# Token stage of a graph and expert network on one core: other softmax batches, VectorE copies, and every third group's down product moved into the first pass

## The reference

```python
logits = x @ gate_w                       # 16 experts
probs = softmax(logits, axis=-1)
scores, tok = top_k(probs.T, 625)         # per expert, over all 10000 tokens
y = (gelu(x[tok] @ w1 + b1) @ w2 + b2) * scores
routed = zeros_like(x).at[tok].add(y)
shared = gelu(x @ sw1 + sb1) @ sw2 + sb2  # hidden size 64
out = routed + shared
```

## Time and profile before

| what | value |
|---|---|
| median of 3 runs | 4557.2 us (4544.28 to 4563.69) |
| profiled execution, its own time | 4542.55 us |
| its span, first to last instruction | 4540.8 us |
| mean granted TensorE clock | 0.912 |
| busy share: TensorE, VectorE, ScalarE, GpSimd | 90%, 62%, 46%, 33% |
| token stage, first pass | 1308.7 to 1470 us |
| token stage, search and second pass | 1475.7 to 1583 us |
| clock granted in the steps / in the search | 0.99 / 0.50 |
| table loads of ScalarE in the stage | 16, of 1283 ns |
| copies of Q by ScalarE | 40, median 357 ns |

### The profile page before, as it was taken

One profiled execution on the slowest core, in us unless ns is written; L12 is line 12 of the kernel. 1 busy time (PEld: TensorE's weight loads), 2 busy tenths in 40 slices (PEclk: granted clock), 3 DMA queues, 4 the chain that ended last, 5 costly groups with the idle time before them and its releaser, 6 DMA issues. The chain is left out here.

```text
span 4540.8 us, 65002 instructions
## 1 busy us (share of the span) xinstructions
PE 4084.8 (90%) x22630; PEld 3319.3 (73%) x22630; DVE 2802.7 (62%) x5418; ACT 2085.5 (46%) x3584; POOL 1497.0 (33%) x1431
## 2 busy tenths in 40 slices
PE   7888999889977968789999999998899998999967
PEld 3447788777766656549988589886699874998844
DVE  5665666569965677568844445443555435557888
ACT  1222233333357334265567533575434764335566
POOL 1442266228820758654400333102332004330010
PEclk9998999999988578799999999998999998999965
DMA  8985488449964879765423655225653237545677
GB/s 308 402 330 178 159 293 267 174 142 376 390 229 146 316 151 178 158 220 158 155 74 116 219 167 158 93 104 164 206 158 113 94 123 238 163 146 145 185 198 211
DMA packets 460260, 886.20 MB, mean 195 GB/s; under 512 B 70660, under 2 KB 111221, under 8 KB 459182
## 3 DMA queue, kind: packets, MB, share of 16 engines
q1 hardware_dynamic: 293498, 524.25, 33.9%
q0 software_dynamic: 90016, 237.51, 18.9%
q10 hardware_dynamic: 76456, 120.69, 7.6%
HBM read 609.61 MB, written 303.62 MB: 201 GB/s over the span
## 5 line engine op out<-in xcount | busy, mean ns | idle before, releaser
L2087 POOL DMA_INDIRECT hidden_agg<-edge_sums,edge_where x316 | 354.1, 1121 | 700.5 <-DVE layer_raw_inner L2174 288.5
L1932 POOL DMA_INDIRECT message_x<-g,edge_partner x120 | 118.1, 984 | 771.3 <-POOLq L150 458.2
L783 PE MATMUL hidden_O<-hidden_xh,layer_hi_inner 128*128 128x256 f32 (+1 forms) x1280 | 368.5, 288 | 0.0
L785 PE MATMUL hidden_O<-hidden_xl,layer_hi_inner 128*128 128x256 f32 (+1 forms) x1280 | 362.3, 283 | 0.0
L784 PE MATMUL hidden_O<-hidden_xh,layer_lo_inner 128*128 128x256 f32 (+1 forms) x1280 | 361.6, 283 | 0.0
L2131 ACT ACTIVATE hT_inner<-hidden_O,hidden_b 128x256 f32<-128x256 f32 (+1 forms) x320 | 124.1, 471 | 335.6 <-PE hidden_O L785 335.6
L783 PE MATMUL root_O<-root_hi,root_xh 128*128 128x512 f32 (+1 forms) x632 | 254.1, 402 | 10.6 <-DVE root_xl L1183 10.6
L783 PE MATMUL output_O<-layer_hi_inner,output_hh 128*128 128x512 f32 (+1 forms) x632 | 250.0, 396 | 1.0 <-DVE output_hl L2268 1.0
L784 PE MATMUL output_O<-layer_hi_inner,output_hl 128*128 128x512 f32 (+1 forms) x632 | 249.6, 395 | 0.0
L785 PE MATMUL output_O<-layer_lo_inner,output_hh 128*128 128x512 f32 (+1 forms) x632 | 249.6, 395 | 0.0
L2277 DVE TENSOR_TENSOR layer_raw_inner<-output_O,output_b2t 128x1024 f32<-128x1024 f32 x80 | 96.9, 1211 | 243.2 <-PE output_O L785 243.2
(11 more groups left out here) (505 smaller groups left out, 12681.0 us busy)
## 6 DMA issues: line engine op xcount, KB each, us to landing
edge_sums<-message_res SPq DMA_DIRECT2D x160, 256.0 KB
layer_raw_inner<-g SPq DMA_DIRECT2D x78, 512.0 KB, 4.1
g<-layer_raw_inner SPq DMA_DIRECT2D x78, 512.0 KB
room<-in_L_gnn_basis SPq DMA_DIRECT2D x30, 1280.0 KB, 13.6
order_basis<-in_L_gnn_basis SPq DMA_DIRECT2D x18, 1280.0 KB, 14.3
edge_sums<-relation_res SPq DMA_DIRECT2D x82, 256.0 KB
order_x<-in_x SPq DMA_DIRECT2D x39, 512.0 KB
normed<-order_y ACTq DMA_DIRECT2D x39, 512.0 KB
```

What stands on the lines that cost most here:

```text
L783: eng.matmul(out, a_hi, b_hi, start=start, stop=False)
L785: return eng.matmul(out, a_hi, b_lo, start=False, stop=stop)
L1932: eng.indirect_dma_start(x[t % R][:, :], None, table, bass.IndirectOffsetOnAxis(ap=ed.partner[1][:, t:t + 1], axis=0)).then_inc(ga[t % R], 16)
L2087: eng.indirect_dma_start(agg[j % R][0:n, :], None, ed.sums[1], bass.IndirectOffsetOnAxis(ap=ed.where[1][0:n, c:c + 1], axis=0)).then_inc(g ...
```

## The change

1. Batches of 8, 8, 8, 8, 5 and 3 groups instead of eight of 5. `after` lets turned probabilities of several groups fall into one step, in order; STEPS falls from 53 to 50.
2. `out`, the copy of Q, is VectorE's, at the end of its step behind `low_units`.
3. The groups 2, 5, ... 35 (FIRST, 12 groups or 24 tiles) get their down product in the first pass: `first_down` in TensorE's step g+4 behind `up`, and `first_sum` in VectorE's step g+5, which adds the residual on the way out of PSUM. SyncE loads residual g in step g+1 and stores y in step g+9. The other 28 groups (55 tiles) follow as before, 8 tiles in steps 42 to 49 and 47 in the iterations: 1 or 2 in each instead of 2 or 3.
4. Six residual buffers instead of eight. The residuals of the second pass are no longer loaded in the last steps, but behind the last store of probabilities.

```diff
-BATCHES = [range(b, b + 5) for b in range(0, NG, 5)]
+BATCHES = [range(a, b) for a, b in zip((0, 8, 16, 24, 32, 37), (8, 16, 24, 32, 37, NG))]
...
-    W, RS = 4, 8
+    W, RS = 4, 6
...
-    STEPS = NG + 8 + len(BATCHES[-1])
-    OWN = [(g, t, n) for g in range(NG) for t, n in tiles_of(g == NG - 1)]
+    STEPS = NG + 7 + len(BATCHES[-1])
+    FIRST = list(range(2, NG - 4, 3))
+    ORDER = FIRST + [g for g in range(NG) if g not in FIRST]
+    NF = len(FIRST)
+    KF = NF * TILES
+    OWN = [(i, t, n) for i, g in enumerate(ORDER) for t, n in tiles_of(g == NG - 1)]
     FROM = NG + 2
     EARLY = STEPS - FROM
-    early_at = lambda r: range(r - FROM, r - FROM + 1) if r >= FROM else range(0)
-    beside = lambda b: range(EARLY + (len(OWN) - EARLY) * b // BITS, EARLY + (len(OWN) - EARLY) * (b + 1) // BITS)
+    early_at = lambda r: range(KF + r - FROM, KF + r - FROM + 1) if r >= FROM else range(0)
+    REST_AT = KF + EARLY
+    beside = lambda b: range(REST_AT + (len(OWN) - REST_AT) * b // BITS, REST_AT + (len(OWN) - REST_AT) * (b + 1) // BITS)
...
+        def added(eng, i):
+
+            if i >= NF:
+                eng.wait_ge(s["y"], i - NF + 1)
+            elif i >= 0:
+                eng.wait_ge(s["ev"], (i + 1) * TILES)
...
                 for r in range(NG):
                     load(r)
...
+                    chosen(1, load_residual)(r)
+                    chosen(9, store)(r)
+                    for i, e in enumerate(done_at):
+                        if r == e + 11 + len(BATCHES[i]):
+                            store_probs(i)
+                for i, e in enumerate(done_at):
+                    if e + 11 + len(BATCHES[i]) >= NG:
+                        store_probs(i)
+                for r in range(NG, NG + 9):
+                    chosen(9, store)(r)
+                for i in range(NF, NF + RS):
+                    load_residual(i)
                 for q in range(2):
                     eng.wait_ge(sp[q], 16 * len(range(q, len(BATCHES), 2)))
                 eng.dma_start(p, probs.rearrange("e (k n) -> (e k) n", k=SUB)).then_inc(s["pld"], 16)
...
+                def first_down(i):
+                    g = ORDER[i]
+                    eng.wait_ge(s["gl"], g + 1)
+                    for t in range(TILES):
+                        at = slice(g * GROUP + t * P, g * GROUP + (t + 1) * P)
+                        wait(eng, s["ev"], (i - 1) * TILES + t + 1)
+                        three(eng, O[t][:, :], gh[:, at], gl[:, at], w2h[:, :], w2l[:, :], True, True).then_inc(s["M"], 1)
...
-                run(lagged(0, turn_rows), lagged(3, turn_logits), after(7, turn_probs), lagged(1, up), early(down))
+                run(lagged(0, turn_rows), lagged(3, turn_logits), after(7, turn_probs), lagged(1, up), chosen(4, first_down), early(down))
...
-                run(lagged(0, high), lagged(2, copy_logits), lagged(2, acts), at_end(5, exps), after(7, out), early(leave))
+                run(lagged(0, high), lagged(2, copy_logits), lagged(2, acts), at_end(5, exps), early(leave))
...
+                def out(g):
...
+                    eng.wait_ge(s["pt"], g + 1)
+                    eng.tensor_copy(pT[i % 2][:, at:at + width(g)], Q[:, 0:width(g)]).then_inc(s["ptc"], 1)
+
+                def first_sum(i):
+                    q = i % W
+                    wait(eng, st[q], i // W * 16)
+                    eng.wait_ge(lr[i % RS], (i // RS + 1) * 16)
+                    for t in range(TILES):
+                        eng.wait_ge(s["M"], i * TILES + t + 1)
+                        eng.tensor_tensor(y[q][:, t, :], O[t][:, :], rsd[i % RS][:, t, :], ALU.add).then_inc(s["ev"], 1)
...
-                run(lagged(4, shift), lagged(0, low), at_end(6, divide), lagged(2, low_units))
+                run(lagged(4, shift), lagged(0, low), at_end(6, divide), lagged(2, low_units), after(7, out), chosen(5, first_sum))
```

More of the change, by code:

```diff
@@ L1269, in after, with turn_ @@
         def after(delay, step):
-            turns = {done_at[i] + delay + k: g for i, b in enumerate(BATCHES) for k, g in enumerate(b)}
-            return lambda r: step(turns[r]) if r in turns else None
+            turns, at = [], 0
+            for i, b in enumerate(BATCHES):
+                for k, g in enumerate(b):
+                    at = max(at, done_at[i] + delay + k)
+                    turns.append((at, g))
+            def turn_(r):
+                for own, g in turns:
+                    if own == r:
+                        step(g)
+            return turn_
         def at_end(delay, step):
@@ L1297, in load, with load_residual, store @@
                     eng.dma_start(part(xin[g % W], last(g)), rows(rows_in, g, last(g))).then_inc(ld[g % W], 16)
[L1299 to L1305, removed]
+                def load_residual(i):
+                    g = ORDER[i]
+                    added(eng, i - RS)
+                    eng.dma_start(part(rsd[i % RS], last(g)), rows(residual, g, last(g))).then_inc(lr[i % RS], 16)
+                def store(i):
+                    g = ORDER[i]
+                    added(eng, i)
+                    eng.dma_start(rows(rows_out, g, last(g)), part(y[i % W], last(g))).then_inc(st[i % W], 16)
                 def store_probs(i):
@@ L1323, in _ @@
                 eng.dma_start(p, probs.rearrange("e (k n) -> (e k) n", k=SUB)).then_inc(s["pld"], 16)
-                for g in range(NG):
-                    store(g)
-                    if g + RS < NG:
-                        load_residual(g + RS)
+                for i in range(NF, NG):
+                    store(i)
+                    if i + RS < NG:
+                        load_residual(i + RS)
                 for q in range(W):
@@ L1334, in _ @@
                 eng.iota(own_i[:, :], [[1, 1]], base=0, channel_multiplier=1).then_inc(s["ibit"], 1)
-                for g in range(NG):
-                    q = g % W
-                    eng.wait_ge(s["ev"], turned(g))
-                    eng.wait_ge(lr[g % RS], (g // RS + 1) * 16)
-                    eng.tensor_tensor(part(y[q], last(g)), part(y[q], last(g)), part(rsd[g % RS], last(g)), ALU.add).then_inc(s["y"], 1)
+                for i in range(NF, NG):
+                    g, q = ORDER[i], i % W
+                    eng.wait_ge(s["ev"], turned(i))
+                    eng.wait_ge(lr[i % RS], (i // RS + 1) * 16)
+                    eng.tensor_tensor(part(y[q], last(g)), part(y[q], last(g)), part(rsd[i % RS], last(g)), ALU.add).then_inc(s["y"], 1)
             @block.tensor
@@ L1453, in _ @@
                 eng.dma_start(b1r[:, :], b1.unsqueeze(1)).then_inc(s["w"], 16)
-                run(lagged(0, high), lagged(2, copy_logits), lagged(2, acts), at_end(5, exps), after(7, out), early(leave))
-                for k in range(EARLY, len(OWN)):
+                run(lagged(0, high), lagged(2, copy_logits), lagged(2, acts), at_end(5, exps), early(leave))
+                for k in range(REST_AT, len(OWN)):
                     leave(k)
```

38 lines of the change are left out of this document (18 added, 20 removed).

## The result

The changed kernel took 4580.95 us as median of 7 runs (4570.23 to 4602.99), the kernel before 4550.24 of 7 (4544.28 to 4563.69): ratio 1.0083, 95% interval 1.0063 to 1.0103. On a second chip, with 12 and 35 runs, the ratio was 1.0043 (1.0022 to 1.0064), 4585.69 against 4565.81 us. (The two medians of the first chip alone give 1.0067, inside the interval.) So it is slower, by 20 us on the second chip and by 31 (medians) or 38 (ratio) on the first. The forecast was 4576, in a range from 4554 to 4600.

What follows compares the result with a forecast made beforehand. A two-step loop from TensorE's transposes to logits and back was the bound. Pass +18.7, clock +2, tail +0.5, load +8, search -9.4, first scan -1 summed to +18.8 us: median 4576, range 4554 to 4600.

Steps and rivals of the forecast that it cites:

- The round: Three token-stage steps, lengthened by down product, VectorE's copy and first sums: 11.74 us instead of 8.82.
- Rival 2: VectorE's copy and sums hide behind TensorE's long step: three steps take 10.2 us, median about 4566; chance 0.19.
- The batches: Four softmax exponentials instead of six between groups 6 and 39 cost 1.3, 0.5, 1.4 and 1.3 us: 4.5.
- The clock: Falls to 0.50 behind the batches of steps 12 and 36, while the old fall goes: +2 us (-2 to +8).
- Rival 1: Regular waits of 1.85 us bring a clock fall of about 2 in each of 11 rounds: 22 more, 4596; chance 0.17.
- Removing it gives nothing: Taking the copy of Q off ScalarE saves nothing, as it stood outside the loop, in time to spare.
- the sentence on the drain: By the skill's drain of 1.38 us per table switch, seven saved loads would give 9.7; the sum left it out.
- Tail: From group 39's transposes to the last copy of Q, 24.4 us before: +0.5 (bounds -5 and +3).
- Load for the search: SyncE's load queues behind two stores and six residual loads, 4.2 MB: some 15 us instead of 7.25, +8.
- Search: 29 intervals with 47 tiles instead of 68, including eight meetings with GpSimd adds: 93.9 us against 104.4, -9.4 in all.
- The ninth meeting: One more meeting of VectorE with a GpSimd add at the end of the search, costing 1.2 us.
- the shorter first scan: The first scan behind the search overlaps a GpSimd add less: -1 us (bounds 0 and -2).

Runs made afterwards that it cites:

- the sums moved: Changed kernel, but each group's first sum made tile by tile in steps g+5 and g+6 between VectorE's low and low_units; ratio 1.0013, group 6 to 39 121.48 us.
- the kernel with the copy back: Changed kernel with the copy of Q on ScalarE again and three stores ahead of other stores of probabilities; group 6 to 39 130.41 us, token stage 285.2.
- the kernel with the copy alone: Kernel before, changed only by putting the copy of turned probabilities (Q) on VectorE; group 6 to group 39 takes 119.48 us.
- the kernel with all together: Changed kernel with sums tile by tile, Q's copy on ScalarE, two search tiles per iteration, residual loads earlier; 4532.01 us against 4547.45 before, ratio 0.9963.
- the kernel with two tiles an iteration: Changed kernel with the search's 47 tiles spread two to an iteration over the first 24 iterations; search 86.2 us, ratio 1.0045.

## Why the prediction was right, and where it was not

The sum, +18.8, meets +20.9 in the stage, and 4576 meets 4580.95. Right within the range, but two of its steps erred, in opposite directions: the pass without falls of the clock came out 2.1 shorter than said, and the falls cost 2 to 4 more.

That the median comes within 5 us is in part luck. The forecast stood on 4557.2, the median of three runs; seven give 4550.24, and from there +18.8 is 4569.0. The medians of the first chip lie 30.7 apart, of which the stage explains some 21. And by the border that the prediction drew at 4580.0, this result counts as slower, to which it gave 0.41, and not as the same (0.55).

*The round.* Right, and now shown part by part. The three steps that the working builds up are 8.71 before; the copy makes them 9.02; with the down product they are 10.40 (the sums moved); with the sums in the loop 11.61. That is +0.31, +1.38, +1.21, where the prediction had 0.34, 1.40 and 1.29, and 11.74 in all. The waits for lg are 1.71 instead of 1.85. Of the first two rounds, said to be 11.40, one took 11.67 and one 10.96. Rival 2, a round of 10.2 because the sums hide, falls; in the other place they do hide.

*The batches.* 4.5 was said, 4.0 came. Where no fall is near, round 12 is 12.41 and round 30 is 12.90 (third profile of after), so 1.4 and 1.3. The batch of step 20 costs nothing: rounds 18 and 21 of the kernel with the copy back are 11.27 and 11.29, like its others. Round 36 is 13.45 in the second profile, but its last 1.1 us are at 0.50, and L to T takes 2.38 there instead of 1.82; without that 12.9, so 1.3. The pass without falls then adds up to 130.5: 11.67 and 10.96 for the first two rounds, six of 11.61, and the three named. The prediction had 132.6.

*The clock.* This step failed, in three ways. "I expect a fall for each, and the old one goes: +2" was a slip of bookkeeping first: 132.6 held no fall while 113.9 held one, so the old one had already gone and two falls of 2 were +4. Second, the price: rounds 24 and 27 of the third profile take 11.87 and 12.87 around one fall instead of 2 x 11.61, so 1.5 and not 2, and only some 0.3 where the fall runs into the batch of step 28 (rounds 27 and 30, 11.89 and 12.89 in the second profile). Third, the count: of six batch waits (2.84 and 3.00 in three profiles) five were followed by a fall, as said; but so were 8 of the 18 regular waits of 1.7, which I had left out. That is 4 to 5 falls, the last of them partly behind the pass in two of the profiles, and 134.4 to 136.8 instead of 130.5: 3.9 to 6.3, at or above the +4 of a correct account, for other reasons.

*Rival 1* was thus half right. Its sign for deciding, more than three of the eleven rounds with 0.50, came in all three profiles. Its price did not: 3.9 to 6.3 instead of 22, since most regular waits pass without a fall and a fall costs less. A wait's length alone does not tell: 1.71 was followed by a fall in none of 15 cases before and in 8 of 18 after, where it comes every 11.6 us; 1.40 (copy back) in none of 6. The Trainium skill, "TensorE: Matmul & The Clock Gate", "What's actually happening", has the clock follow how busy the engine has been recently; that the same 1.71 goes either way agrees with it. What tells the waits with a fall from those without, no run here shows.

*"Removing it gives nothing."* Wrong for ScalarE's copy: behind each batch it held Q for 0.87. The gain is hidden in the sum, since the copy's price on VectorE takes it back (in the kernel with the copy alone both together leave 0.2 over all rounds without a new fall). The seven table loads that the sentence on the drain counts as saved are six: 16 before, 10 after.

*Tail* +0.5: +0.9. *Load for the search* +8: +8.3; moving the loads takes the wait to 9.3, which shows the queue as its cause. *Search* 93.9: 93.5 to 93.6, with eight meetings as counted, and intervals of 2.78 and 2.98. The ninth meeting (+1.2) and the shorter first scan (-1) lie behind the last compare; from there to TensorE's first matmul on the scan's result are 8.65 before and 9.15 after, +0.5.

*Outside the stage* I had forecast nothing. The first profile put 35 us there, 23 of them one low stretch, and the first chip's ratio (38 us) is above the stage's 21, the second's (20) is not. The median of before alone was 4550, 4566 and 4547 us on three chips. So the part outside the stage was no error of a step, but it bounds how well a forecast of this kernel's median can do.

## What to carry to other kernels

When work moves onto an engine that stands in a loop between two others, its place in that engine's step is worth more than its length: ask which instruction's result the partner waits for, and put the new work behind it. Count a regular wait of TensorE twice, once for itself and once for the clock falls that may follow it (here 8 of 18 waits of 1.7, none of 6 of 1.4), and keep a fall in or out of both sides of a comparison. A small load on which everything waits belongs ahead of the bulk transfers on its queue, but look at what then stands behind them; and when work runs beside a chain on two engines that exclude each other, when each piece starts matters more than how much there is.

## What of the hardware I had not expected

- The granted clock falls behind a wait in some cases and not in others at equal length (1.71: 0 of 15 and 8 of 18), for about 3 us at 0.50 each time; one fall costs 1.5 us, about half its length, or some 0.3 where it runs into a batch's wait.
- Long stretches at 0.50 occurred in the first message phase of one profile each of after (54.6 us), of the kernel with the sums moved (44.4) and of the kernel with all together (51.2), in the first with TensorE busy throughout: 120.6 us for a phase that otherwise takes 97.
- The length of a GpSimd add (2.35) hardly changes when it meets VectorE's keep (2.35 where they meet, 2.37 where they don't); the whole price falls on VectorE (0.16 becomes 1.35 to 1.64) as long as the add began first. The other way round GpSimd pays: behind the search of the kernel before, VectorE's scan (two SBUF inputs) is under way when the add of the last group begins, and that add takes 3.71, where it takes 1.25 in the kernel with two tiles an iteration:

```profile
1586.18 4.87 DVE L1541 TENSOR_TENSOR_SCAN tokens_scan<-tokens_eq 128x1250 f32<-128x1250 f32 x1
1588.39 3.71 POOL L1339 TENSOR_TENSOR tokens_y<-tokens_y,tokens_rsd 16x512 f32<-16x512 f32 x1
```
